# Attention steps of a unit in another order: the three far key blocks placed between the steps near the diagonal

## What is computed

```python
att = jnp.einsum('bhqd,bhkd->bhqk', q, k) * (1.0 / math.sqrt(D))
att = att + rel_bias                      # depends on q - k only; constant from a distance of 128 on
att = jnp.where(causal[None, None], att, -jnp.inf)
att = jax.nn.softmax(att, axis=-1)
y = jnp.einsum('bhqk,bhkd->bhqd', att, v)
...
x = _layernorm(x + y @ W_proj.T + b_proj)
x = _layernorm(x + ffn(x))                # two experts by top-1 routing, and a shared expert
```

## Time and profile before

| | |
|---|---|
| median of 3 runs | 987.3 us (985.47 to 989.46) |
| the profiled execution, its own time | 986.67 us |
| its span in the profile | 984.9 us |
| the attention stage in it | 158.5 to about 480 us |
| PE busy over the span | 840.3 us (85%) |
| ACT busy | 568.3 us (58%) |
| DVE busy | 556.4 us (56%) |
| mean granted clock of PE | 0.935 of full speed |

### The profile page before, as it was taken

The page is one execution under the profiler, slowest core; times in us unless marked ns, Lnnn a source line. Parts: engine busy times, 40 slices in busy tenths (PEclk is TensorE's granted clock), DMA queues, the critical chain, the costliest instruction groups (busy, mean ns, idle before and its releaser), DMA issues. The chain is left out here.

```text
span 984.9 us, 18061 instructions
## 1 busy us (share of the span) xinstructions
PE 840.3 (85%) x6689; PEld 600.2 (61%) x6689; DVE 556.4 (56%) x1160; ACT 568.3 (58%) x733; POOL 252.7 (26%) x200
## 2 busy tenths in 40 slices
PE   7269926999998799999678899889996999999993
PEld 5157712343333333333367888779886999998993
DVE  3348864665765465566587756674552355445543
ACT  4247725888888688888634453453342445454451
POOL 4224431000100100020145452444142233333333
PEclk9679966999999799999989999999998999999997
DMA  7785557566856565593291111111036444443301
GB/s 154 91 295 189 177 128 134 114 112 107 125 97 111 93 114 96 100 136 54 52 248 55 55 55 55 44 50 60 22 142 227 158 163 151 151 151 132 127 23 43
DMA packets 61806, 112.96 MB, mean 115 GB/s; under 512 B 9412, under 2 KB 50409, under 8 KB 56297
## 3 DMA queue, kind: packets, MB, share of 16 engines
q1 hardware_dynamic: 56824, 99.07, 43.2%
q0 software_dynamic: 4896, 12.73, 3.5%
HBM read 58.15 MB, written 30.82 MB: 90 GB/s over the span
## 5 line engine op out<-in xcount | busy, mean ns | idle before, releaser
L873 ACT ACTIVATE probs<-slots 128x1024 f32<-128x1024 f32 x288 | 275.0, 1031 | 49.2 <-DVE slots L942 39.9
L942 DVE TENSOR_TENSOR slots<-slots,bias_t 128x512 f32<-128x512 f32 (+1 forms) x288 | 159.2, 604 | 77.8 <-PE slots L975 75.9
L1644 DVE TENSOR_TENSOR h_lo<-h_f,h_hi 128x512 fp32r<-128x512 f32 x136 | 104.6, 771 | 129.7 <-PE o_ps L1742 78.8
L993 PE MATMUL o_ps<-probs,v_st 128*32 128x256 f32 (+1 forms) x2560 | 155.5, 365 | 0.8 <-ACT probs L873 0.8
L993 PEld LDWEIGHTS o_ps<-probs,v_st 128*32 128x32 f32 x2560 | 67.5, 110 | 77.8 <-issue 48.8
L975 PE MATMUL slots<-q_first,k_st 99*128 99x512 bf16 (+3 forms) x384 | 83.5, 343 | 31.6 <-DVE v_st L887 16.0
L1484 ACT ACTIVATE h_f<-slots,b_cur 128x512 f32<-128x512 f32 x72 | 49.5, 688 | 102.6 <-PE slots L1728 91.6
L1484 ACT ACTIVATE h_f<-slots,b_c 128x512 f32<-128x512 f32 x64 | 44.0, 687 | 95.6 <-PE slots L1728 94.0
L1488 ACT ACTIVATE h_hi<-h_f 128x512 fp32r<-128x512 f32 x136 | 86.0, 632 | 4.3
L975 PE MATMUL slots<-q_second,k_st 99*128 99x512 bf16 (+3 forms) x384 | 80.5, 329 | 7.7 <-ACT probs L873 7.7
L1045 POOL TENSOR_TENSOR y_t<-y_t,rs_row 128x2048 f32 (+1 forms) x4 | 18.2, 4562 | 258.5 <-DMA rs_row<-rsum_d 258.5
(11 more groups left out here) (207 smaller groups left out, 1889.8 us busy)
## 6 DMA issues: line engine op xcount, KB each, us to landing
qk_d<-parts SPq DMA_DIRECT2D x32, 384.0 KB, 2.6
cur_hi<-experts_hi SPq DMA_DIRECT2D x9, 1024.0 KB, 4.8
cur_lo<-experts_lo SPq DMA_DIRECT2D x9, 1024.0 KB, 7.2
k_st<-qk_d SPq DMA_DIRECT2D x16, 384.0 KB
q_first<-qk_d SPq DMA_DIRECT2D x48, 128.0 KB
q_second<-qk_d SPq DMA_DIRECT2D x48, 128.0 KB
xs_sb<-xs_d SPq DMA_DIRECT2D x9, 528.0 KB, 5.1
bs_sb<-base_d SPq DMA_DIRECT2D x9, 512.0 KB, 4.0
```

The costliest lines, as they stand in the source:

```text
L873: nc.scalar.activation(probs[:, k % PBUFS, :, 0:w], slots[:, k % SLOTS, :, 0:w], ACT.Exp).then_inc(exped, 1)
L942: ins = dve.tensor_tensor(tile, tile, bias_t[:, h0:h0 + 2, first:first + w], ALU.add)
L993: ins = pe.matmul(o_ps[32 * j2:32 * j2 + 2 * D, half, q:q + w], v_st[:, g, j, j2, :], probs[:, (k + j2 // 2) % PBUFS, j2 % 2, col:col + w] ...
L1644: dve.tensor_tensor(h_lo[:, n % 3], h_f[:, q % 2], h_hi[:, n % 3].bitcast(F32), ALU.subtract).then_inc(hl_ok, 1)
```

## The change

The three far steps of a unit, which stood in a row behind step 2, are now placed one by one between near steps. The key blocks, their sizes and their number are the same. The two tables, one step per place (N near, F far; the block is half/key block):

| place | 0 | 1 | 2 | 3 | 4 | 5 | 6 | 7 | 8 |
|---|---|---|---|---|---|---|---|---|---|
| before | 0/0 N | 0/1+0/3 N | 0/2+1/6 N | 1/0 F | 1/1 F | 1/2 F | 1/3 N | 1/4 N | 1/5+1/7 N |
| after | 0/0 N | 0/1+0/3 N | 1/0 F | 0/2+1/6 N | 1/1 F | 1/3 N | 1/2 F | 1/4 N | 1/5+1/7 N |

The places of DVE's other work move too: the first-half copy from behind (4, 0) or (5, 1) to behind (6, 0) or (6, 1), the packing from (3, 1) to (4, 1), and the reciprocal from (5, 0) to (4, 0).

```diff
-STEPS = [[x] for x in WHOLE[0]] + [[WIDE[0], NARROW[0]]]
-STEPS += [[MIDDLE[0], MIDDLE[1][:4] + (TT // 2,)]]
-STEPS += [[x] for x in WHOLE[1]] + [[WIDE[1], NARROW[1]]]
+FAR = [[x] for x in WHOLE[1] if TT * x[0] - P * x[1] >= 2 * P]
+CLOSE = [[x] for x in WHOLE[1] if [x] not in FAR]
+STEPS = [[x] for x in WHOLE[0]] + [[WIDE[0], NARROW[0]]] + FAR[0:1]
+STEPS += [[MIDDLE[0], MIDDLE[1][:4] + (TT // 2,)]] + FAR[1:2]
+STEPS += CLOSE[0:1] + FAR[2:3] + CLOSE[1:2] + [[WIDE[1], NARROW[1]]]
...
-        EVAC1, EVAC0, EVAC0_FIRST, REST, INVERT = (1, 1), (4, 0), (5, 1), (3, 1), (5, 0)
+        EVAC1, EVAC0, EVAC0_FIRST, REST, INVERT = (1, 1), (6, 0), (6, 1), (4, 1), (4, 0)
```

## The result

| | before | after |
|---|---|---|
| median | 986.4 us (22 runs, 983.0 to 989.5) | 990.5 us (22 runs, 987.4 to 995.2) |
| ratio to before, 95% interval | | 1.0042 (1.0028 to 1.0056) |
| profiled execution / its span | 986.67 / 984.9 us | 990.43 / 988.7 us |
| first to last exponential | 159.2 to 478.7 us | 158.9 to 482.0 us |

The changed kernel is slower, by 4.1 us. That lies inside the bound of 0.5% for the median (the interval reaches 0.56%), and inside the range. Nearly all of the difference of the two spans, 3.8 us, is in the attention: its exponentials take 323.1 us instead of 319.5, and from the start of the last of them to the end it takes 506.7 instead of 506.2.

What follows compares the result with a forecast made beforehand. PE and ACT pace the attention; three slots cost PE 1.58 us per unit. Terms −0.75 + 2.2 + 0.3 = +1.75 us gave 988.4 us for the execution; median forecast 988.7 (+1.4), range 984 to 993.

Steps and rivals of the forecast that it cites:

- The waits belong to slots, and the additions' chain is what PE waits for.: PE in the attention: three slots; chain from scores through addition and exponential 2.44 us, PE back at the slot after 2.41.
- Ordinary units: 15 x −.05 = −.75.: Fifteen ordinary units: losses .75 + .05 become .61 + .14 at places 4 and 5; −0.75 us, ends 0 and −1.5.
- Reciprocal in front of place 5's additions: +1.1 in each of two batches.: First units of second and fourth batch: additions queue behind a reciprocal awaiting the sums' DMA; +2.2 us, ends 0 and +4.
- additions that wait longer for the reciprocal than 1.5 us: Place 5 in the second and fourth batch: sign that the sums' DMA depends on the order, proving the forecast wrong.
- First unit of all, +.3.: First unit: no copy stands before its additions, so the two-block step has less to win; +0.3 us, ends 0 and +0.4.
- The third batch, 0.: Loop's jump: sums arrive inside PE's 8.71 us standstill, so nothing is added; 0, ends ±0.8 us.
- Each loss belongs to the additions of one step and three slots, not to how many near steps stand in a row.: PE's losses in a unit, 1.58 us in sum at four places: rule that runs of near steps do not matter.
- That the additions are hidden by far steps: Attention: far steps cover near steps' additions; four losses go, 962 us; weaker form, two-block loss only, 978; chance for both 0.06.
- The slower one, a reciprocal that blocks longer: First units of batches: sums arrive later, DVE blocked longer; decides at 1.8 us, +5.4; 2 us gives 993; chance 0.09.

Runs made afterwards that it cites:

- kernel 4: Changed kernel with the reciprocal behind place 6 and PE's outputs in halves, between the two pairs of scores: 994.8 us, ratio 1.0084 to the kernel before.
- kernel 5: Kernel before without the second wide addition of the two-block step (bias of block 1/6 left out): 977.3 us, one run.
- kernel 6: Changed kernel without the second wide addition of the two-block step (bias of block 1/6 left out): 976.7 us, one run.
- kernel 1: Changed kernel with the reciprocal moved from behind place 4 to behind place 6: 986.5 us, ratio 1.0001 to the kernel before.
- kernel 11: Changed kernel with the loop over batches written out and the reciprocal moved behind place 6: 977.0 us, ratio 0.9916 to the kernel before.
- kernel 9: Kernel before with the attention's loop over batches written out: 975.2 us, ratio 0.9888 to the kernel before.
- kernel 8: Changed kernel with the attention's loop over batches written out: 981.3 us, ratio 0.9952 to the kernel before.
- kernel 2: Kernel before with the second-half copy behind the two-block step, first units' first-half copy and reciprocal also later: 992.7 us, ratio 1.0067.
- kernel 3: Opposite of the change: the three steps with two additions side by side, against the kernel before: 968.8 us, ratio 0.9818.
- kernel 7: Kernel 3 with the third unit's loads ahead of the spreading of the inverted sums: 975.6 us, ratio 0.9890 to the kernel before.

## Why the prediction was right, and where it was not

- *The waits belong to slots, and the additions' chain is what PE waits for.* Right, and shown by kernels 4, 5 and 6. The starts of an ordinary unit outside the loop came as worked out: 19.31 us, waits of .65 and .14 at places 4 and 5 (forecast .61 and .14).
- *Ordinary units: 15 x −.05 = −.75.* Outside the loop −.09 each; inside it +.06 to +.34. For the twelve units of the table the term measured +.2. The step left out that the batches do not all run in the same form: I read one unit, in the first batch and at the start of the second, and took the loop's units for the same, though they took 19.48 us and not 19.40 before.
- *Reciprocal in front of place 5's additions: +1.1 in each of two batches.* In the profiled execution +.69 and +1.46, together +2.2 as forecast. By the medians its place costs 4.0 ± 2.2 us (kernel 1) and 3.5 ± 2.5 (kernel 11); both intervals hold the 2.2, and whether it costs more than that is open. The arrival was taken as steady from two rows, 7.40 and 7.43; that they agreed was chance. It was 6.97 and 7.82 after, and in kernel 9, with DVE's order of before, 8.32, 7.30 and 8.10. Lateness is paid in full (kernel 8), while sums that come early enough are worth nothing more.
- *The sign "additions that wait longer for the reciprocal than 1.5 us".* It came up, with 1.9 us in the fourth batch, and does not mean what it was to mean: the forecast itself had 1.47, and the arrivals of the two orders overlap (7.3 to 8.3 us in kernel 9, 6.3 to 7.8 in the changed kernel and 8), so that the sums' DMA depends on the order is not shown.
- *First unit of all, +.3.* It was +.96. By its rows, the head start of PE, which had hidden the two-block step, was not in the sum.
- *The third batch, 0.* +.32, within its ends.
- *"Each loss belongs to the additions of one step and three slots, not to how many near steps stand in a row."* The first half holds; the second is wrong where the steps have two additions. Kernel 2 (.40 lost behind the two-block step, for .79 in the changed kernel) and kernel 3 (−.77 per unit) show that neighbours share a pause. The change pulled the two-block step out of such a row: it lost the sharing, .39, and gained the copy's .48, which leaves the .09 measured. The prediction worked this small gain out correctly from the starts and drew the wrong rule from it.
- *The rivals.* That the additions are hidden by far steps fell: ACT still waits 36.0 us for DVE, after 39.9. The slower one, a reciprocal that blocks longer, named the right mechanism; its delay varied but reached at most .9 us (8.32 in kernel 9), not the 1.8 that it asked for.

The sum was +1.75 us for the execution and came to +3.8; the median moved by +4.1, where +1.4 was forecast. The units' account has +3.6, and the 1.9 us above the sum stand in three terms: 1.0 in the ordinary units, .7 in the first unit of all, .3 in the third batch. The mechanism of a unit was right. That the time still fell inside 984 to 993 is in part the width of that range, since the sum had half the size.

## What to carry to other kernels

When the profile shows an engine waiting for another that is often idle, work out the chain through one buffer, with the time in which the waiting engine comes back to it, before spreading the work: with the three slots here, heavy steps next to each other shared one pause, and spread out each paid its own. When an order changes, look at what else stands in that engine's queue (here a reciprocal that waits for a DMA) and at what another queue holds behind it (here SyncE's loads). Read more than one repetition of a loop body: first, last and middle ones can be different programs. And compare one profile with another stage by stage: here the stage that nobody had touched varied by 6.7 us between executions, more than the change was worth.

## What the runs showed of the hardware that was not expected

- After PE had waited 2.21 and 1.72 us (kernel 6) or 2.83 us (kernel 2), the granted clock was .57 in the 4 us that follow (249 to 253, 413 to 417, 275 to 279 us), near the lower level (1.2 GHz), though PE was busy there again; after a wait of 1.37 us in the changed kernel and a pause of 1.27 in kernel 3 it was 1.00 (2.4 GHz). In kernel 6 this cost 1.6 us each time on top of the wait.
- Changing PE between scores (99 rows, full width) and outputs (32-column tiles) once more per step cost .25 us there and back.
- At the loop's jump PE stood still for 8.7 us before, 8.8 after, 9.6 in kernel 1, 8.6 in kernels 2 and 5, 7.8 in kernel 3, 6.6 in kernel 4, 8.3 in kernel 6, and not at all in the profiled execution of kernel 7. Behind it the granted clock of the kernel before was .55 from 320 to 330 us, near the lower level, .94 in the 10 us behind and 1.00 after; 16 output matmuls took 1.94 us there for 1.07.
- Kernel 3 lost 1.3 us in the middle of a row of matmuls without a semaphore in sight, just after 4 us in which the DMA engines were busy all the time (share 1.04 from 400 to 404 us); written out, the same order has no such pause in its one trace.
